# A gather pipeline on GpSimd, before and after two waits for landing per block

## The reference

```
h = embed(x)                                   # rows of a table, padding masked
h = h + toeplitz_attention(layernorm(h))       # convolutions by FFT, gates
h = h + product_key_attention(layernorm(h))    # below
h = h + attention(layernorm(h))                # one head
h = h + mixture_of_experts(layernorm(h))       # 8 experts, top 2
```

```
k = einsum('bnhk,bnhkd->bnhd', kv_scores, keys_table[ind])
v = einsum('bnhk,bnhkd->bnhd', kv_scores, values_table[ind])
```

## Time and profile before

| | us |
|---|---|
| median of 3 runs | 3272.53 |
| lowest and highest | 3261.38, 3274.84 |
| span of the profiled execution | 3918.3 |
| TensorE busy in it | 3008.9 (77%) |
| VectorE busy | 2785.8 (71%) |
| ScalarE busy | 2039.4 (52%) |
| GpSimd busy | 2057.7 (53%) |

### The profile page before, as it was taken

How to read it: one execution, slowest core, us unless ns; L and a number is a source line. 1 busy time by engine, 2 the same in 40 slices (tenths; PEclk the granted TensorE clock), 3 DMA queues, 4 the chain that set the end, 5 groups by cost and what they waited for, 6 DMA issues and landing times.

```text
span 3918.3 us, 39268 instructions
## 1 busy us (share of the span) xinstructions
PE 3008.9 (77%) x9722; PEld 1391.1 (36%) x9722; DVE 2785.8 (71%) x9999; ACT 2039.4 (52%) x4498; POOL 2057.7 (53%) x2095
## 2 busy tenths in 40 slices
PE   4861657878787878878778868888778878888888
PEld 2430223333333333333333433333333433333343
DVE  7678777777777777776777887777768786874433
ACT  3231545555555555655555655556555655555532
POOL 3011666666656665555565655556656655655400
PEclk8985777888787888989888989888888988989899
DMA  1001121212121111112121212111111212121100
GB/s 37 22 8 52 44 66 43 62 45 57 48 56 47 52 52 50 52 46 55 44 59 38 65 40 57 44 52 53 51 50 46 57 46 56 42 62 39 33 3 3
DMA packets 85626, 179.86 MB, mean 46 GB/s; under 512 B 40177, under 2 KB 41107, under 8 KB 85398
## 3 DMA queue, kind: packets, MB, share of 16 engines
q0 software_dynamic: 66560, 135.40, 13.1%
q1 hardware_dynamic: 18838, 41.94, 3.5%
HBM read 176.15 MB, written 1.05 MB: 45 GB/s over the span
## 4 chain that ended last, share of the span: by engine, by line
PE 41%; DVE 25%; another core or an unknown queue 11%; issue 8%; ACT 8%; ACTq 0%; DVEq 0%
PE mx_acc L1430 12%; PE mx_O L1442 7%; PE mx_area L1476 6%; DVE mx_W L1787 5%; PE mx_D L1420 4%; ACT mx_GT L1691 3%; DVE mx_KVs L2013 3%; PE mx_area L1456 2%; ACT mx_W L1623 2%; DVE mx_mx_part L2031 2%; PE mx_area L1492 1%; DVE mx_mx L2031 1%; PE mx_X L1560 1%; PE mx_area L1486 1%
## 5 line engine op out<-in xcount | busy, mean ns | idle before, releaser
L1402 POOL DMA_INDIRECT mx_G<-in_kv_table,mx_slot_i x2048 | 2004.0, 978 | 1394.6 <-issue 590.1
L1430 PE MATMUL mx_acc<-mx_W,mx_table 128*128 128x512 f32 x2048 | 1180.7, 660 | 1.6 <-ACT mx_kvT L1630 0.7
L1787 DVE SCALAR_TENSOR_TENSOR mx_W<-mx_D,mx_W 128x512 f32<-128x512 f32 x1024 | 699.1, 683 | 297.5 <-ACT mx_W L1623 180.5
L1623 ACT ACTIVATE mx_W<-mx_D 128x512 f32<-128x512 f32 x1024 | 606.6, 593 | 523.2 <-PE mx_D L1420 231.0
L1691 ACT ACTIVATE mx_GT<-mx_G,mx_slot_w 128x128 f32<-128x128 f32 x2048 | 759.2, 495 | 3.2 <-DVE mx_KVs L2013 1.1
L1420 PE MATMUL mx_D<-mx_U,mx_pick_b 96*128 96x512 bf16 x1024 | 432.7, 423 | 110.8 <-DVE mx_W L1787 52.5
L1430 PEld LDWEIGHTS mx_acc<-mx_W,mx_table 128*128 128x128 f32 x2048 | 436.1, 214 | 201.9 <-issue 104.5
L1647 ACT ACTIVATE mx_PT<-mx_area 128x512 f32<-128x512 f32 x472 | 241.8, 514 | 464.9 <-PE mx_area L1480 146.3
L1442 PE MATMUL mx_O<-mx_PT,mx_KVs 128*65 128x512 f32 (+3 forms) x768 | 347.5, 536 | 170.0 <-ACT mx_PT L1647 82.8
L1456 PE MATMUL mx_area<-mx_KTa,mx_QTa 64*128 64x512 f32 (+3 forms) x384 | 200.6, 607 | 132.6 <-DVE mx_mx L2031 66.1
L2013 DVE TENSOR_REDUCE mx_KVs<-mx_GT 128x128 f32<-128x2048 f32 x128 | 291.9, 2280 | 6.0 <-ACT mx_GT L1691 5.9
(11 more groups left out here) (390 smaller groups left out, 4462.4 us busy)
## 6 DMA issues: line engine op xcount, KB each, us to landing
mx_table<-in_kv_dense SPq DMA_DIRECT2D x64, 512.0 KB
mx_G<-in_kv_table,mx_slot_i POOLq DMA_INDIRECT x2048
tz_table<-in_c_dft SPq DMA_DIRECT2D x1, 2048.0 KB
tz_table<-in_c_idft SPq DMA_DIRECT2D x8, 256.0 KB, 2.6
out_h<-mx_xc SPq DMA_DIRECT2D x4, 256.0 KB
mx_G<-in_c_pick SPq DMA_DIRECT2D x1, 528.0 KB
st_h<-in_tok_W,em_ids POOLq DMA_INDIRECT x32
st_keys<-in_pk_keys SPq DMA_DIRECT2D x1, 512.0 KB, 3.9
```

The costliest lines, as they stand in the source:

```text
L1402: pool.indirect_dma_start(G[g % RING][:, r, :], None, a["kv_table"], bass.IndirectOffsetOnAxis(slot_i[n % 2][:, k, r:r + 1], 0))\
L1430: pe.matmul(acc[:, :], table[:, tile, :], W[c % TILE_RING][:, :], start=(tile == 0), stop=(tile == TILES - 1)).then_inc(applied, 1)
L1623: act.activation(W[c % TILE_RING][:, :], D_ps[c % 3][:, :], ACT.Exp).then_inc(p_done, 1)
L1787: dve.scalar_tensor_tensor(W[c % TILE_RING][:, :], D_ps[c % 3][:, :], 0.0, W[c % TILE_RING][:, :], ALU.is_ge, ALU.mult).then_inc(w_done, 1)
```

## The change

One constant is added, and one wait in the loop of the gathers. `r` is the rank of a gather in its block, `k` the block in its pair, `g` the block in all. At `r = 0` (all blocks but the first) GpSimd waits until all 16 gathers of the block before have landed, at `r = 8` until the first eight of its own have.

```diff
 RING = 2
+LANDED = 8
 TILE_RING = 6
...
                     if r % 2 == 0 and ahead > 0:
                         pool.wait_ge(w_done, ahead)
+                    if r % LANDED == 0 and (g or r):
+                        before = NB * n + k - (r == 0)
+                        pool.wait_ge(gathered[before % RING], 16 * (TOPK * (before // RING) + (r or TOPK)))
                     pool.indirect_dma_start(G[g % RING][:, r, :], None, a["kv_table"],
                                             bass.IndirectOffsetOnAxis(slot_i[n % 2][:, k, r:r + 1], 0))\
                         .then_inc(gathered[g % RING], 16)
```

## The result

The kernel with the two waits takes 3744.8 us (median of 4 runs, 3739.5 to 3750.2) against 3271.8 us (4 runs): ratio 1.145, 95% interval 1.1426 to 1.1474, 473 us slower. The forecast was 3446 us with a range to 3530. In the kernel after, lines of the mixer have moved down by four: the gather is L1406, the new wait L1405, the weighing L1695, the mask L1791.

What follows compares the result with a forecast made beforehand. GpSimd was taken to be about as full as TensorE in a run. 255 waits at 1.1 us add 281 us, less 107 us spare: 3272.5 + 174 = 3446 us; range for 8 in 10, 3235 to 3530.

Steps and rivals of the forecast that it cites:

- What bounds it: In unprofiled runs' gather stretch, GpSimd was said to be about as full as TensorE, needing 2618 us of 2700 to 2794.
- the 646 us: Profiled span over the runs' median, 645.8 us; taken from the gather stretch alone (2700 us left) or all stretches alike (2794).
- The price of one wait: At 255 first and ninth gathers: landing plus restart less the usual step, 0.98 to 1.23 us, 1.1 taken, 281 us in all.
- The spare: GpSimd's idle time in a run's gather stretch that could absorb added waits: 60 to 154 us, 107 taken.
- 3918 stays 3918: Claim that the profiled span, 3918 us, would not change, since added waits are given back from other waits there.
- the late signals: In the gather stretch, TensorE's signals arrive late while gathers run; the chain's unknown-queue share, some 431 us, mostly absent from runs.
- where the waits vanish in others: Argument for the hidden case: in the profiled execution, the added waits disappear inside other waits of GpSimd.
- Hidden: Rival: gathers cost less without the profiler, say 1.1 us, so the added 281 us fit; 3272 us, chance 0.22.
- half of it: Rival: first gathers' wait stays covered by waiting for ScalarE, only 141 us added; 3272 to 3353, middle 3307, chance 0.13.
- Faster: Rival: draining the queue at every ninth gather lets TensorE's late signals through, 43 us gained; 3230 us, chance 0.18.
- That a wait could be met at no cost: Rival: the added waits are met already, if a landing beats the 0.30 us step; no chance worth giving.
- a drain dearer than any row above: At the added waits, a drain costing more than any profile row cited; left outside the 8-in-10 range, above 3530 us.

Runs made afterwards that it cites:

- The split kernel with met waits: Kernel before with separate landing semaphores per half buffer, plus waits at first gathers for landings eight gathers further back and at ninth ones likewise; 3250.9 us, ratio 0.9940.
- the kernel run again: The kernel before, unchanged, run and profiled a second time; 3277.3 us in one run.
- The kernel with the carried wait: Changed kernel without mask waits at first and ninth gathers, so the ninth gather itself carries its landing wait; 3659.9 us, ratio 1.1202.
- the one with a gather in flight: Kernel before with split semaphores, seven and nine gathers; the ninth gather waits for the first seven only; 3320.7 us, ratio 1.0156.
- the halves: Kernel before with only one of the two waits added: ninth gathers only 3472.4 us (ratio 1.0628), first gathers only 3465.7 us (1.0614).
- the one with four by block: Kernel before with four landing semaphores, one for each block in turn, no wait added; 3252.1 us, ratio 0.9952.
- split alone: Kernel before with a separate landing semaphore for each half buffer, no wait added; 3250.5 us, ratio 0.9934.

## Why the prediction was wrong

**What bounds it: right.** That GpSimd is nearly full in a run was derived from 0.978 + 0.30 us a gather and a stretch of 2700 to 2794 us. Measured, the stretch is 2722 us (334.2 to 3056.4), a gather 0.979 us, and the steps 0.30 us. The split kernel with met waits has a stretch of 2704 us. So of the two ways to share out the 646 us, the first, all from the gather stretch, was the right one. The Trainium skill (Perfetto Trace Analysis, "Identifying the Most-Contended Engine") calls the engine with the highest occupancy the most contended. Here that rule misled: in the kernel run again GpSimd is busy for 63% of the span, VectorE for 84%, and yet 473 of the 523 us that were added on GpSimd came out at the end.

**The price of one wait: here it failed.** The step put it at 0.98 to 1.23 us, 1.1 taken; it is 2.05 us. Two parts are missing. (a) The landing was read as the moment when the DMA engines fall quiet, 1.01 to 1.26 us after the gather. That part holds: the last packet ends 1.24 us after a gather's issue (median) in the trace after as well. But the last count comes 1.58 us after (median). (b) The restart was read from a gather that waited for a mask, 0.27 us. That is right for a gather that carries its wait: 0.26 us in the kernel made for it. The added wait does not ride on the gather, because the gather has another wait already; it is an instruction ahead, and from the last count to the gather's start it is then 0.76 to 0.79 us. The kernel with the carried wait and the one with a gather in flight show both parts separately. 1.58 + 0.77 - 0.30 = 2.05 us. The step also said that a gather which lands early still costs its 0.27 us; the met waits cost nothing.

**The spare: too large.** 60 to 154 us were allowed, 107 taken. Swallowed were 50 us by the change, 51 and 59 by the halves and 28 in the kernel with one gather in flight. The kernel run again shows why it is so little: between its first and its last gather GpSimd stands idle 718 us (601.7 + 90.1 + 26.4), of which the steps are 624 (2047 at 0.305 us), the first mask's wait 14, and 28 the pauses of the last section, which stay in the changed kernel. That leaves 52 us to give back. The account closes: in the kernel after, the waits cost 543 us beyond a step (by means; the medians give 523), less the 52, less 17 since the gathers' issues got shorter (1987 us for 2004), and 5 for longer pauses make 479, and the gather stretch grew by 478 (3200 for 2722). 255 x 0.95 us for the price and 57 us for the spare make the 299 us by which the forecast was missed; this split uses the 50 us that the total itself gives; the halves and the 52 us of the trace are the independent measures.

**The profiled execution: wrong.** "3918 stays 3918" took the late signals of the earlier trace rows as a habit of profiled executions. The kernel run again and the one after have none. In the chain after, TensorE's products by the output weights and VectorE's use of them follow at once (start, length, what):

```profile
1507.45 0.85 PE mx_X L1564 x8
1508.31 0.02 issue
1508.33 0.20 DVE mx_rz L2058
```

0.02 us, where the earlier trace rows have 9.0. The inference that the runs do not hold that time was sound; but the same odd trace supplied "where the waits vanish in others", the main argument for the rival that carried 0.22.

**The rivals.** Hidden (3272) and half of it (3307) fall with the two halves, each of which cost 6%. Faster (3230) falls with its cause: there were no held-up signals to free. That a wait could be met at no cost is true of an earlier landing, not of this one.

**The range.** It left out above 3530 "a drain dearer than any row above", and that is what came. Its upper end rested on two rows that both measured less than the thing priced: a transfer's end in place of its count, and a wake-up of a gather that carries its own wait.

**A rival that the prediction did not have: TensorE's clock.** Its granted clock in the gather stretch was 0.94 in the kernel run again and is 0.87 in the window of the profile after:

```profile
333.00:3524.00 3191.00, 2570.22 (x8361) 1186.20 (x8362) 2428.79 (x9135) 1850.42 (x4185) 1979.50 (x2041) 0.87 0.19 53
```

TensorE is 174 us longer busy there (2570 against 2397), and it stands still 621 us, against 326. GpSimd's time adds up without it. Of the 1213 us that GpSimd stands idle between its first and its last gather, 624 are steps, 543 what the first and ninth gathers wait beyond a step (by means), 35 the pauses of the last section and 12 the wait for the first mask. That leaves nothing for a wait on TensorE's work, so the lower clock did not set the time. Why it fell stays open; no run held it fixed.

## What to carry to other kernels

A wait for the landing of one's own last transfer costs from the end of the issue to the last count, and then the restart of the engine's instructions, here 0.26 us or 0.76 us: price it from a row where an engine was released by that count, and look whether the instruction can carry the wait or another one has to. An engine that issues small transfers can be full at a busy share of 63%, because the step between two is in no share. Before a prediction leans on a profile whose span is far from the runs, only those of its rows should be used that do not depend on what made it long.

## What was not expected

In the kernel before, GpSimd pauses for some 2 us ahead of every 112th gather, always "issue", and always at the second gather of every seventh block. From the kernel run again:

```profile
490.46 0.95 POOL L1402 DMA_INDIRECT mx_G<-in_kv_table,mx_slot_i  x1 [0.30 <-issue]
493.48 0.94 POOL L1402 DMA_INDIRECT mx_G<-in_kv_table,mx_slot_i  x1 [2.07 <-issue]
```

There are sixteen of full length in that trace and eighteen in the one after; at 1.75 us over the step the sixteen are 28 us, at 1.95 us the eighteen are 35. All kernels with two semaphores and sixteen gathers a block have these pauses; the four with split semaphores and the one with four by block have none. Nor has the kernel with twelve gathers a block, which has two semaphores: its longest "issue" wait is 0.7 us. So two semaphores alone do not bring the pauses. The longest "issue" wait of GpSimd was 2.4 us in the kernel run again and this with four semaphores (split alone; us, times, longest):

```profile
POOL mx_G L1402 <- issue: 568.7, 1866, 0.3
```

Four semaphores in place of two bring 16 to 22 us of it. What makes GpSimd pause after 112 gathers stays open; nothing but the semaphores was varied for it.
